# A graph layer's softmax: scores and maxima turned by TensorE into one bank, the exponential taken there, two gates made by POOL

## What is computed

```python
scores = jnp.einsum('ehd,ehd->eh', Q[dst], mod_k) / D ** 0.5
seg_max = jax.ops.segment_max(scores, dst, num_segments=N)
ex = jnp.exp(scores - seg_max[dst])
denom = jax.ops.segment_sum(ex, dst, num_segments=N)
w = ex / denom[dst]
agg = jax.ops.segment_sum(w[:, :, None] * V[src], dst, num_segments=N)
```

## Time and profile before

| | us |
|---|---|
| median of 3 runs | 2440.83 |
| lowest and highest | 2439.93 to 2443.38 |
| the profiled execution's own time | 2438.15 |
| its span in the profile | 2436.4 |
| TensorE matmuls busy | 1969.0 (81%) |
| VectorE busy | 1799.0 (74%) |
| ScalarE busy | 869.7 (36%) |
| POOL busy | 1456.7 (60%) |
| granted TensorE clock, mean share | 0.902 |

### The profile page before, as it was taken

How to read it: one execution, slowest core, us unless ns; L and a number is a source line. 1 busy time by engine, 2 the same in 40 slices (tenths; PEclk the granted TensorE clock), 3 DMA queues, 4 the chain that set the end, 5 groups by cost and what they waited for, 6 DMA issues and landing times. The chain is left out here.

```text
span 2436.4 us, 50363 instructions
## 1 busy us (share of the span) xinstructions
PE 1969.0 (81%) x11356; PEld 1408.1 (58%) x11357; DVE 1799.0 (74%) x3100; ACT 869.7 (36%) x2796; POOL 1456.7 (60%) x1360
## 2 busy tenths in 40 slices
PE   8965777776777777777757999999889999679996
PEld 4533444554554544444545777777655555468885
DVE  6877999999999999999967888878776764321111
ACT  4532111111111111111116777777445555432221
POOL 4655777777777777777732777777654542023442
PEclk9987888888888888888878999999899999889998
DMA  6658999999999999999996888888534643464450
GB/s 218 222 177 275 359 362 358 361 360 354 360 362 355 363 356 359 358 358 360 349 231 205 304 277 278 280 278 277 170 130 169 219 159 119 172 232 168 154 186 36
DMA packets 388111, 649.78 MB, mean 267 GB/s; under 512 B 40235, under 2 KB 235951, under 8 KB 387925
## 3 DMA queue, kind: packets, MB, share of 16 engines
q1 hardware_dynamic: 200132, 277.43, 34.7%
q0 software_dynamic: 77824, 262.55, 30.2%
q10 hardware_dynamic: 110096, 109.07, 12.8%
HBM read 471.00 MB, written 178.83 MB: 267 GB/s over the span
## 5 line engine op out<-in xcount | busy, mean ns | idle before, releaser
L721 POOL DMA_INDIRECT s_kv<-kv_d,s_index x832 | 791.3, 951 | 266.0 <-issue 238.0
L1362 PE MATMUL a_sum_ps<-a_w,a_is_dst 128*128 128x260 f32 x1760 | 403.6, 388 | 20.5 <-DVE sums L1333 11.9
L1275 POOL TENSOR_TENSOR a_w<-a_v,a_w 128x512 f32<-128x512 f32 x220 | 299.1, 1365 | 164.8 <-ACT a_w L1232 107.5
L1362 PEld LDWEIGHTS a_sum_ps<-a_w,a_is_dst 128*128 128x128 f32 x1760 | 328.2, 191 | 95.8 <-issue 25.1
L867 PE MATMUL s_q_ps<-q,s_is_dst 128*128 x2496 | 366.9, 304 | 10.0 <-DVE s_key L776 8.7
L820 PE MATMUL s_mv_ps<-s_mixed 128*128 128x128 f32 x416 | 106.4, 436 | 272.2 <-DVE s_mixed L756 272.2
L771 DVE TENSOR_TENSOR s_key<-s_kv,s_rel_ps 128x1024 f32<-128x1024 f32 x208 | 253.3, 1218 | 63.0 <-issue 36.4
L867 PEld LDWEIGHTS s_q_ps<-q,s_is_dst 128*128 128x128 bf16 x2496 | 253.3, 107 | 79.2 <-issue 12.7
L1248 ACT ACTIVATE a_w<-a_v,a_w 128x64 f32<-128x64 f32 x1100 | 285.8, 335 | 3.5 <-DMA a_v<-v_d 3.5
L1309 DVE SCALAR_TENSOR_TENSOR a_is_dst<-node_of,first_node,a_col_ps 128x256 f32<-128x256 f32 x440 | 208.8, 475 | 82.7 <-PE a_sum_ps L1362 64.9
L781 DVE TENSOR_REDUCE s_part<-s_key 128x16 f32<-128x1024 f32 x208 | 253.7, 1220 | 10.7
(11 more groups left out here) (310 smaller groups left out, 2941.4 us busy)
## 6 DMA issues: line engine op xcount, KB each, us to landing
a_v<-v_d SPq DMA_DIRECT2D x440, 256.0 KB, 3.7
v_d<-s_kv ACTq DMA_DIRECT2D x208, 512.0 KB
s_local<-local_d SPq DMA_DIRECT2D x106, 256.0 KB, 6.0
xh_d<-h_hid SPq DMA_DIRECT2D x24, 1024.0 KB, 7.5
s_kind<-type_d SPq DMA_DIRECT2D x212, 64.0 KB, 6.6
s_kv<-kv_d,s_index POOLq DMA_INDIRECT x832
kv_d<-pkv SPq DMA_DIRECT2D x50, 256.0 KB, 2.0
wd<-in_L_ffn_Wd SPq DMA_DIRECT2D x8, 1024.0 KB, 12.0
```

What stands on the lines that cost most here:

```text
L721: nc.gpsimd.indirect_dma_start(out=kv[:, g * GROUP + b, :], out_offset=None, in_=R["kv"], in_offset=bass.IndirectOffsetOnAxis(ap=index[:, ...
L1275: nc.gpsimd.tensor_tensor(heads(w[:, at, mine, 0:C]), heads(v[:, g, mine, :]), w[:, at, mine, C:, None].broadcast_to([P, len(tiles), H, D] ...
L1362: ins = nc.tensor.matmul(sum_ps[(g * PAIRS + k) % BANKS][:], is_dst[:, g % WRING, 2 * k + u, :], w[:, g % WRING, 2 * k + u, :], start=(u = ...
```

## The change

POOL makes `in_first` and `in_last` behind its IOTA, and VectorE waits for both only ahead of the heads. VectorE no longer subtracts. ScalarE writes `minus`, the identity times -1, as its first instruction. TensorE makes products 7 to 11 in one row behind the carries, and then for each bank four fp32 matmuls of score times the identity (`begin`), which open an accumulation, and four of maximum times minus the identity, which close it: score minus maximum stands in the bank, turned. ScalarE takes the exponential out of the bank straight into `M["scores"]`, all eight of them. `begin` of banks 4 to 7 waits until the exponential of the bank's earlier use is out. The products' copies all stand ahead of the exponentials on ScalarE.

```diff
+        minus = sb("m_minus", [TS_ROWS, TS_ROWS])
...
@@ gpsimd
             pool.wait_ge(S["node_set"], 1)
+            for j, (gate, at) in enumerate(((in_first, 0), (in_last, W - 1))):
+                nc.gpsimd.tensor_scalar(gate[:], seg[:], seg[:, at:at + 1], None, ALU.is_equal).then_inc(S["outer_set"], 1)
+                pool.wait_ge(S["outer_set"], 2 * j + 1)
+                nc.gpsimd.tensor_scalar(gate[:], gate[:], -1.0, BIG, ALU.add, ALU.mult).then_inc(S["outer_set"], 1)
@@ tensor
-            for i in range(7, 10):
+            for i in range(7, 12):
                 product(i)
 
-            pe.wait_ge(S["copied"], n_bank)
-            for b in range(n_bank):
-                pe.wait_ge(S["exp_ready"], b // 2 + 1)
+            def shifted(b, x, eye, first):
+                for j in range(4):
+                    c = 4 * (b % 2) + j
+                    ins = nc.tensor.matmul(bank[b % 4][:, j, 0:TS_ROWS], x[:, b // 2, c * P:(c + 1) * P], eye,
+                                           start=first and j == 0, stop=not first, skip_group_check=True)
+                return ins
+
+            def begin(b):
                 if b >= 4:
                     pe.wait_ge(S["back"], b - 3)
-                for j in range(4):
-                    c = 4 * (b % 2) + j
-                    ins = nc.tensor.transpose(bank[b % 4][:, j, 0:TS_ROWS], score[:, b // 2, c * P:(c + 1) * P],
-                                              M["ident"][0:TS_ROWS, 0:TS_ROWS])
-                ins.then_inc(S["back_turned"], 1)
-                if b in (1, 3):
-                    product(10 + b // 2)
+                shifted(b, score, M["ident"][0:TS_ROWS, 0:TS_ROWS], True)
+
+            pe.wait_ge(S["copied"], n_bank)
+            pe.wait_ge(S["minus_set"], 1)
+            for b in range(4):
+                begin(b)
+            for h in range(H):
+                pe.wait_ge(S["steps"], M["softmax_steps"] + 2 * (h + 1))
+                for b in (2 * h, 2 * h + 1):
+                    shifted(b, most, minus[:], False).then_inc(S["back_turned"], 1)
+                if h + 2 < H:
+                    begin(2 * h + 4)
+                    begin(2 * h + 5)
@@ scalar
+            nc.scalar.activation(minus[:], M["ident"][0:TS_ROWS, 0:TS_ROWS], ACT.Copy, scale=-1.0).then_inc(S["minus_set"], 1)
...
-            for i in range(8):
+            for i in range(2 * len(MIXED)):
                 mixed(i)
...
-            for h in range(H):
-
-                act.wait_ge(S["steps"], M["softmax_steps"] + 3 * (h + 1))
-                nc.scalar.activation(score[:, h, :], most[:, h, :], ACT.Exp).then_inc(S["exp_ready"], 1)
-                if h == 0:
-                    mixed(8)
-                    mixed(9)
-                else:
-                    back(2 * h - 2)
-                    back(2 * h - 1)
-                    if h < H - 1:
-                        mixed(9 + h)
+                nc.scalar.activation(view[:, b // 2, c:c + 4, :], bank[b % 4][:, :, 0:TS_ROWS], ACT.Exp).then_inc(S["back"], 1)
@@ vector
-            st.mark(nc.vector.tensor_scalar(in_first[:], seg[:], seg[:, 0:1], None, ALU.is_equal))
-            then(nc.vector.tensor_scalar(in_last[:], seg[:], seg[:, W - 1:W], None, ALU.is_equal))
-            st.mark(nc.vector.tensor_scalar(in_first[:], in_first[:], -1.0, BIG, ALU.add, ALU.mult))
-            then(nc.vector.tensor_scalar(in_last[:], in_last[:], -1.0, BIG, ALU.add, ALU.mult))
...
+            dve.wait_ge(S["outer_set"], 4)
             for h in range(H):
...
-                then(nc.vector.tensor_tensor(most[:, h, :], score[:, h, :], most[:, h, :], ALU.subtract))
-            view = M["scores"][:].rearrange("p r (c h) -> p h c r", h=H)
-            for b in (n_bank - 2, n_bank - 1):
-                dve.wait_ge(S["back_turned"], b + 1)
-                c = 4 * (b % 2)
-                nc.vector.tensor_copy(view[:, b // 2, c:c + 4, :], bank[b % 4][:, :, 0:TS_ROWS]).then_inc(S["back"], 1)
...
-        M["softmax_steps"] = 41
+        M["softmax_steps"] = 37
```

More of the change, by code:

```diff
@@ L924, in stage_softmax @@
         mixed_out = [sem(f"x_mixed_out{w}") for w in range(2)]
-        names = "mixed_done mixed_copied items_in mix_in zeroed sums_zeroed node_set paired vw_done vw_copied z_done z_read steps turned copied ends_turned ends_ready carry_turned exp_ready back_turned back"
+        names = "mixed_done mixed_copied items_in mix_in zeroed sums_zeroed node_set paired vw_done vw_copied z_done z_read steps turned copied ends_turned ends_ready carry_turned back_turned back minus_set outer_set"
         S = {n: sem("m_" + n) for n in names.split()}
@@ L1061, in _ @@
             view = M["scores"][:].rearrange("p r (c h) -> p h c r", h=H)
-            def back(b):
+            for b in range(n_bank):
                 act.wait_ge(S["back_turned"], b + 1)
                 c = 4 * (b % 2)
-                nc.scalar.copy(view[:, b // 2, c:c + 4, :], bank[b % 4][:, :, 0:TS_ROWS]).then_inc(S["back"], 1)
-            for h in range(H):
-                act.wait_ge(S["steps"], M["softmax_steps"] + 3 * (h + 1))
-                nc.scalar.activation(score[:, h, :], most[:, h, :], ACT.Exp).then_inc(S["exp_ready"], 1)
-                if h == 0:
-                    mixed(8)
-                    mixed(9)
-                else:
-                    back(2 * h - 2)
-                    back(2 * h - 1)
-                    if h < H - 1:
-                        mixed(9 + h)
+                nc.scalar.activation(view[:, b // 2, c:c + 4, :], bank[b % 4][:, :, 0:TS_ROWS], ACT.Exp).then_inc(S["back"], 1)
             act.wait_ge(S["back"], n_bank)
```

## The result

| us | before | after |
|---|---|---|
| median | 2441.04 (11 runs, 2439.09 to 2443.38) | 2447.29 (11 runs, 2445.23 to 2451.28) |
| the profiled execution, its span | 2438.15, 2436.4 | 2447.38, 2445.6 |
| stage, from VectorE's first instruction to the last write of the exponentials | 48.65 | 53.78 |

The ratio is 1.0024 with a 95% interval of 1.0017 to 1.0032, that is 4.2 to 7.8 us more; 2446.7 was predicted. Of the 9.2 us between the two spans 2.5 lie ahead of the stage (it starts at 1270.29 instead of 1267.76, behind unchanged instructions), 5.1 in it and 1.5 behind it. Four more profiles on one chip, all with the same instructions ahead of the stage, start it between 1269.4 and 1273.7, and the unchanged stretch behind it, from VectorE's first instruction there, took 1119.4 to 1123.3 us over all the profiles. So the outer two terms are variation, and the change itself is worth the 5.1.

What follows compares the result with a forecast made beforehand. VectorE was taken to set the softmax stage's end, with TensorE's matmuls late after the change. Front -2.3 + 3.0 and tail +5.2 make +5.9 us on the median of 2440.83: 2446.7 us, range 2442.0 to 2452.0.

Steps and rivals of the forecast that it cites:

- First scan: Start of the stage: with the gates off VectorE, the first scan starts at 1270.33, 2.32 us saved.
- Gates on POOL: Front: POOL gates and VectorE scans alternate, a gate ending 1.0 us past the release; four cost 3.0 us, net +0.7.
- Rival 2: Front: no exclusion between scans and gates, the carry gains 1.75 us; +3.4, 2444.3 us; chance 0.10.
- Middle: From the ends to the turned carries: sequence as today, ends at 1293.2 instead of 1292.54, carries turned at 1297.3.
- The tail on TensorE: Behind the carries: sixteen calls of 8 x 0.112 us, 14.3 us, against 2.9 for 32 transposes before.
- rival 1: TensorE's tail: matmuls at column pace, 0.09 instead of 0.112 us; +3.2, 2444.0 us; chance 0.09.
- rival 4: TensorE's tail: an fp32 identity matmul runs as one instruction of 0.09 us; -1.8, 2439.0 us; chance 0.05.
- The tail on ScalarE: Exponentials out of the bank take 0.91 us alone, 0.73 behind another; TensorE waits 0.36 twice; end at 1322.3.
- The clock: TensorE's idle ahead of the ends becomes 3.1 us; if the clock falls there, 1 to 3 us more.
- rival 3: Front dearer: gates at 2.3 us, +10.8, or clock falling in the longer idle, +7 to +9; around 2450; chance 0.14.
- Sum: Whole change: -2.3 + 3.0 at the front and +5.2 in the tail, together +5.9 us; median 2446.7.

Runs made afterwards that it cites:

- c_no_reads: The changed kernel with both gates filled by POOL memsets, which read nothing, and the comparison left out; stage end at +51.85 us, against 53.78.
- e_transposes: The changed kernel with its 64 fp32 identity matmuls replaced by transposes, scores left out, on the second chip; stage end at +49.17 us, against 53.78.
- e_again: The kernel of e_transposes run once more, on the third chip; stage end at +49.17 us, tail 19.11, whole 2708.88 (before 2706.90).
- d_gates_late: The changed kernel with POOL making the real gates only after ends_ready, behind the scans; stage end at +53.51 us, against 53.78.

## Why the prediction was right

- **First scan** at 2.32 us earlier: right, 2.26.
- **Gates on POOL**, "Each blocked the other for the whole instruction", 1.0 us past the release. For the add and multiply this was right: they took 0.84 past the release, and the scan behind each ended 2.13 us after POOL's end (1281.24 - 1279.11), where 2.17 was predicted. For the `is_equal` the step failed in both parts, and the two errors cancelled. It took 2.65 past the release, beyond the upper bound of 2.3. But the scan was held 0.55 us and ended only 0.39 us after POOL's end (1278.27 - 1277.88); held to the end of the `is_equal` by the same rule, each of two scans would have lost another 1.7 us, and the front would have cost 3.4, by an estimate from these rows. The four holds are 2.28 us instead of 3.0, so net 0.0 instead of +0.7: a better front than predicted, by luck. The rule of the Trainium skill (SBUF — State Buffer, Who interferes with whom) agrees with the scans behind the add and multiply, and with `c_no_reads` in that a scan is free beside a POOL instruction that reads nothing; that the two exclude each other whole is not what the scans beside the `is_equal` show. The gates were done at 1285.16, 14.5 us ahead of L1137, so their length was covered as said.
- **Rival 2** (no exclusion): not what happened, but `c_no_reads` made its case, and gained 1.93 where the rival had 1.75.
- **Middle**: 4.04 us from the ends to the carries, as before.
- **The tail on TensorE**: right. 128 instructions at 0.111 (0.112 predicted); rival 1 (0.09) and rival 4 (one instruction) did not occur, and `e_transposes` shows that the number of instructions and their pace are the price. Rival 4's own end of 46.9 us was too early by 2.3: 0.5 of that are the carries, late by the clock, and the rest the waits for banks that it left out. The rule of four passes for true fp32 (Trainium skill, FP8 and Floating Point Precision, TensorE Precision Notes), which gave an estimate of 173 ns a matmul, is not what the rows show for 104 columns: 0.22 us. For the products' 256 columns four passes at 2.4 GHz would be 0.427 us, an estimate by the same rule, and there the trace agrees: two instructions of 0.22.
- **The tail on ScalarE**: an exponential out of the bank takes 0.89 alone (0.91 predicted). The last four follow each other every 0.89 us because TensorE closes a bank in 8 x 0.111 us; where TensorE is faster, in `e_again`, they follow every 0.70 (0.73 predicted). Two stalls of TensorE were 0.25 and 0.26 (0.36 each predicted). Tail 24.94, predicted 25.0.
- **The clock** stayed full behind the 2.70 us idle in the profile of `after`; on the other chips rival 3's second half happened ahead of the ends, at 1.7 us, within the price of 1 to 3. Before was not profiled there, so whether its clock falls too is not shown; the whole was 5.3 us longer than before on the third chip, less than the 7 to 9 that the rival adds up to.
- **Sum**: stage +5.13 instead of +5.9; median +6.25, of which the interval, 4.2 to 7.8, holds both. That the median of 2447.29 lies within 0.6 us of the prediction is in part luck: the front came 0.7 cheaper, and about 1 us lies outside the stage, where nothing was changed.

## What to carry to other kernels

Before giving VectorE's elementwise pass to TensorE, count the instructions of an fp32 matmul: at 104 columns an identity multiply that accumulates costs two of 0.11 us where a transpose costs one of 0.09. Here TensorE's share of the turning grew from 2.9 to 14.2 us, five times as much, and work that was hidden on the engine with slack became the bound. Split such a change over the two engines and open accumulations where TensorE idles, rather than moving all of it. Before sending a small operation to POOL, try to make it shorter where it is.

## What was not expected

- POOL's `is_equal` by a scalar per partition over 1024 fp32 took 2.87 and 2.96 us with the scans out of the way, its add and multiply 1.05, its memset 0.96; VectorE's took 0.69 to 0.77.
- Though the `is_equal` ran 2.65 us beyond the release, the scan beside it was held only 0.55 us. Beside the first `is_equal` in `d_gates_late` (1296.50 to 1299.37) four VectorE instructions with two inputs (L1116 to L1120), up to 1298.43, kept their 0.25 us, and then L1121 and L1122, with one input each, were held to its end, by about 0.7 us; beside the second (from 1300.60) L1125 was free and L1129 was held by 0.65. L1124 was held to the end of the add and multiply. So the `is_equal` holds VectorE for a part of its time only; which part, and why, stays open.
- The clock fell behind idles of 1.93, 2.08, 2.18 and 2.28 us on the second and third chip, and stayed full behind 2.45 and 2.70 in the profiles of before and `after`, and behind 2.47 and 2.60 on the first chip. It is not the chip alone: in `e_again` it stayed full behind an idle of 2.79 us at the start of the stage (granted 1.00 from 1534.7 to 1538.4) and fell behind one of 2.08 later. The length of the idle does not tell; what does stays open.
